# A Swin attention block on one core: other Gelu piece sizes and hidden buffers in its last stage, and output additions moved to GpSimd

## The chip, the cores and the metric

The kernel runs on one core of a Trainium2 chip. The metric is the device time of one execution in microseconds (us). The profile of one execution gives, beside it, the span from the first to the last instruction, and every instruction's start and duration. Engines are called by their short names: PE is TensorE (PEld its weight load), ACT is ScalarE, DVE is VectorE, POOL is GpSimd, SP is the engine that issues nearly all transfers.

## The reference

The input is 8 images of 16 x 128 tokens with 32 channels. The block is one layer of a shifted-window transformer:

```python
y = roll(layernorm(x, g1, b1), (-2, -2))          # then windows of 4 x 32 tokens
q, k, v = (xw @ qkv_w + qkv_b)                     # 4 heads of 8
attn = softmax(q k^T * scale + bias + mask)
x = x + unroll((attn v) @ proj_w + proj_b)
z = layernorm(x, g2, b2)
z = gelu(z @ fc1_w + fc1_b) @ fc2_w + fc2_b        # 32 -> 128 -> 32
return x + z
```

The last three lines, for each image, are what the end stage computes.

## The kernel before

X holds the whole input as 128 partitions (the tokens of a window) by 8 images of 512 columns (16 windows x 32 channels). Attention runs over 64 pairs of windows (8 an image). Every engine has its own instruction list, written out by hand, and executes it in order; semaphores order the engines against each other. The second layer norm and the MLP follow.

The second norm of an image is: row sums (`sums`, L471), a mean (L477), `center` (L495, `xc` = X - mean), `square` (`sq`), sums of squares (L483), a variance (L489), `power` on POOL (L376, var ^ -0.5), `scale` (`yn` = `xc` * `rstd`, L504 on DVE, L386 on POOL) and `channels_second` (L563, a 32 x 32 block transpose into `yT2`). Images 0 to 6 are normalized while attention still runs. Image 7 can be normalized only after its last attention output is added: `add_attention(15)` (L546), which follows PE's `tokens_first(15)` (L1018), DVE's `normalize` and `copy_onT`, and PE's `channels_first(15)` (L1024) and `project_out(15)` (L1030). The number is that of an octet of windows, two octets an image.

The end stage, for image m:

- `fc1(m)` (L951): four matmuls on PE, each one row group of 32 partitions into a PSUM bank of 512 columns, so 2048 hidden columns. Three pairs of banks (`ps1`, `pq`, `ps2`) take turns as halves of 1024 columns. It waits for the Gelu of the first half of image m-1.
- `gelu(m, half)` (L735): ACT reads a pair of banks and writes 1024 columns of `hT[m % 2]`, one of two hidden buffers in memory that attention used before (`q_rows`, `k_rows`). It is preceded once by a table load.
- `fc2(m)` (L967): four matmuls on PE into one bank, `pav` for even and `pch` for odd images; for image 7 two halves of 256 columns into `pq`.
- `mlp_tokens(m)` (L552): DVE transposes the bank into `m_tok`, a single buffer.
- `add_residual(m)` (L558): DVE adds X (which POOL's `add_mlp_bias`, L411, has made X + fc2_b) into `res[m % 2]`, one of two output buffers.
- SP writes `res` to memory (L318, image 7 in halves at L321). `add_residual(m)` waits until the transfer of image m-2 has landed (`d_out[m % 2]`).

PE's order at the end is: `tokens_first(15)`, `fc1(1)`, `channels_first(15)`, `fc2(0)`, `project_out(15)`, `fc1(2)`, `fc2(1)`, then `fc1(m)`, `fc2(m-1)` for m from 3 on. DVE's is: `mlp_tokens(0)` and the normalization of image 7, with `add_residual(0)` and `mlp_tokens(1)` in its middle where it waits for POOL's square; then transpose and addition of one image after the other, `channels_second(7)` behind image 3.

Of the kernel before, what the change touches and what calls it, by code (L numbers as in the profile page):

```python
# [28 lines left out]
LEAD = 4  # L29
AV_LAG = 2  # L30
NPROB = 4


_WIDTHS = dict(g1=1, b1=1, qkb=1, qks=1, colscale=128, wqk=128, ident=128, id3=32,
# [9 lines left out]
def swin_kernel(nc, x, params, rel_i_in, rel_j_in, aux_in, scratch, rel_scratch, out):  # L44
# [3 lines left out]
    with ExitStack() as ctx:  # L48
        def sb(name, shape, dt=fp32):
            return ctx.enter_context(nc.sbuf_tensor(name, shape, dt))  # L50

        def sem(name):
            return ctx.enter_context(nc.semaphore(name))
# [49 lines left out]
        rec = sb("rec", [128, 32])  # L103
        onorm = sb("onorm", [128, 256])
        onT = sb("onT", [128, 256])
        m_tok = sb("m_tok", [128, 512])
        res = sb("res", [128, 2, IMG])

        hT = [t[:, 2, :].bitcast(fp32) for t in (q_rows, k_rows)]

        def psum(name, cols):
            return ctx.enter_context(nc.psum_tensor(name, [128, cols], fp32))

        ps1, ps2, pq = psum("ps1", 1024), psum("ps2", 1024), psum("pq", 1024)
        pav, pch = psum("pav", 512), psum("pch", 512)
        Q0, Q1 = pq[:, 0:512], pq[:, 512:1024]
        FC1 = (ps1, pq, ps2)

        def first_home(j):
            return ps2 if j in (1, 3) else ps1  # L120

        def mlp_home(m, lo):
            return (pav, pch)[m % 2] if m < B - 1 else (Q1 if lo else Q0)


        d_x = [sem(f"d_x{b}") for b in range(B)]
# [27 lines left out]
        onTp_done, onT_done, proj_done, x2_done = (sem("onTp_done"), sem("onT_done"), sem("proj_done"),  # L154
                                                   sem("x2_done"))
        fc1_done, gelu_done, fc2_done = sem("fc1_done"), sem("gelu_done"), sem("fc2_done")
        mtok_done, res_done = sem("mtok_done"), sem("res_done")

        rel_raw, rel_rest = prob[:, 2, 0:512], prob[:, 3, 0:512]

# [2 lines left out]
        def after(eng, s, count):  # L163
            if count > 0:
                eng.wait_ge(s, count)
# [39 lines left out]
        def _(sp):  # L205
# [108 lines left out]
                        gather(n, MID, 0)  # L314
                        gather(n, MID, 1)
            for m in range(B - 1):
                sp.wait_ge(res_done, m + 1)
                sp.dma_start(out[:, m * IMG:(m + 1) * IMG], res[:, m % 2, :]).then_inc(d_out[m % 2], 16)  # L318
            for half in range(2):
                sp.wait_ge(res_done, B + half)  # L320
# [7 lines left out]
        def _(pool):  # L328
# [125 lines left out]
                if p == PAIRS:  # L454
                    add_mlp_bias(B - 2)

            square(second_norm(B - 1))
            power(second_norm(B - 1))
            scale(second_norm(B - 1))
            add_mlp_bias(B - 1)  # L460


        @block.vector
        def _(dve):
# [67 lines left out]

            def normalize(q):
                dve.wait_ge(otok_done, q + 1)
                o = pch[:].rearrange("p (n c) -> p n c", c=16)
                after(dve, on_done, q)
                dve.reciprocal(rec[:].unsqueeze(2), o[:, :, HD:HD + 1]).then_inc(rec_done, 1)
                dve.wait_ge(rec_done, q + 1)
                dve.tensor_tensor(onorm[:].rearrange("p (n d) -> p n d", d=HD), o[:, :, 0:HD],
                                  rec[:].unsqueeze(2).to_broadcast([128, 32, HD]), ALU.mult).then_inc(on_done, 1)  # L540

            def add_attention(q):
                dve.wait_ge(proj_done, q + 1)
                dve.wait_ge(xpb_done, q // 2 + 1)
                xs = img(q // 2).rearrange("p (g t c) -> p t g c", g=NG, t=GW)[:, 2 * (q % 2):2 * (q % 2) + 2]
                dve.tensor_tensor(xs, xs, pch[:, 0:256].rearrange("p (t g c) -> p t g c", t=2, g=NG),  # L546
                                  ALU.add).then_inc(x2_done, 1)

            def mlp_tokens(m, lo=0, hi=512):
                dve.wait_ge(fc2_done, m + 1 + lo // 256)  # L550
                after(dve, res_done, m)
                dve.transpose(m_tok[:, lo:hi], mlp_home(m, lo)[:, lo:hi]).then_inc(mtok_done, 1)  # L552

            def add_residual(m, lo=0, hi=512):
                dve.wait_ge(mtok_done, m + 1 + lo // 256)
                dve.wait_ge(xmb_done, m + 1)
                after(dve, d_out[m % 2], 16 * (m // 2))
                dve.tensor_tensor(res[:, m % 2, lo:hi], m_tok[:, lo:hi], img(m)[:, lo:hi], ALU.add).then_inc(res_done, 1)  # L558

            def channels_second(m):  # L560
                i, seq = second_norm(m)
# [66 lines left out]
            def copy_onT(q):  # L628
                dve.wait_ge(onTp_done, q + 1)
                dve.wait_ge(proj_done, q)  # L630
                dve.tensor_copy(onT[:], pch[:, 0:256]).then_inc(onT_done, 1)

            for p in range(PAIRS):
                b, s = p // PPI, p % PPI
# [34 lines left out]
            copy_oT(OCTETS - 1)  # L669
            normalize(OCTETS - 1)  # L670
            copy_onT(OCTETS - 1)
            mlp_tokens(0)
            add_attention(OCTETS - 1)
            dve.wait_ge(x2_done, OCTETS)
            means(second_norm(B - 1), B - 1)
            center(second_norm(B - 1), B - 1)
            add_residual(0)
            mlp_tokens(1)
            variances(second_norm(B - 1))
            add_residual(1)  # L680
            for m in range(2, B - 1):
                mlp_tokens(m)
                add_residual(m)
                if m == B - 5:
# [7 lines left out]
        def _(act):  # L692
# [39 lines left out]
            def gelu(m, half):  # L732
                act.wait_ge(fc1_done, 2 * m + half + 1)
                after(act, fc2_done, m - 1)
                act.activation(hT[m % 2][:, 1024 * half:1024 * (half + 1)], FC1[(2 * m + half) % 3][:], ACT.Gelu,  # L735
                               bias=f_bias[:]).then_inc(gelu_done, 1)

            act.dma_start(par[:, 0:PSPLIT], params[:, 0:PSPLIT]).then_inc(d_par[0], 16)
            act.wait_ge(zero_ready, 1)
# [75 lines left out]
                    square(second_norm(b - 1))  # L815

            for m in range(B):
                gelu(m, 0)
                gelu(m, 1)


        @block.tensor
        def _(pe):
# [115 lines left out]
            def fc1(m):  # L939
                pe.wait_ge(yT2_done, m + 1)  # L940
                if m == 0:
                    pe.wait_ge(max_done, PAIRS)
                    pe.wait_ge(mmid_done, GROUPS)
                    pe.wait_ge(va_done, B)
                else:
                    pe.wait_ge(gelu_done, 2 * m - 1)
                if m == 1:
                    pe.wait_ge(exp_done, PAIRS)
                for wx in range(GW):
                    bank = FC1[(2 * m + wx // 2) % 3][:, 512 * (wx % 2):512 * (wx % 2 + 1)]  # L950
                    mm = pe.matmul(bank, w1[32 * wx:32 * (wx + 1), :], yT2[32 * wx:32 * (wx + 1), m, :], start=True,  # L951
                                   stop=True)
                    if wx % 2 == 1:
                        mm.then_inc(fc1_done, 1)

            def fc2(m):
                pe.wait_ge(gelu_done, 2 * m + 2)
                if m == 0:
                    pe.wait_ge(oT_done, OCTETS)
                elif m == 1:  # L960
                    pe.wait_ge(x2_done, OCTETS)
                elif m < B - 1:
                    pe.wait_ge(mtok_done, m - 1)
                parts_of = ((0, 512),) if m < B - 1 else ((0, 256), (256, 512))
                for lo, hi in parts_of:
                    for wx in range(GW):
                        mm = pe.matmul(mlp_home(m, lo)[32 * wx:32 * (wx + 1), lo:hi], P("w2"),  # L967
                                       hT[m % 2][:, 512 * wx + lo:512 * wx + hi], start=True, stop=True)
                    mm.then_inc(fc2_done, 1)

            pe.wait_ge(w_ready, 1)
# [42 lines left out]
            def tokens_first(q):  # L1014
                pe.wait_ge(oT_done, q + 1)
                after(pe, x2_done, q)
                for u in range(4):
                    mm = pe.transpose(pch[:, 128 * u:128 * (u + 1)], oT[:, 128 * u:128 * (u + 1)], P("ident"))  # L1018
                mm.then_inc(otok_done, 1)

            def channels_first(q):
                pe.wait_ge(on_done, q + 1)
                for t in range(2):
                    mm = pe.transpose(pch[:, 128 * t:128 * (t + 1)], onorm[:, 128 * t:128 * (t + 1)], P("ident"))  # L1024
                mm.then_inc(onTp_done, 1)

            def project_out(q):
                pe.wait_ge(onT_done, q + 1)
                for t in range(2):
                    mm = pe.matmul(pch[:, 128 * t:128 * (t + 1)], onT[:, 128 * t:128 * (t + 1)], P("wp"),  # L1030
                                   start=True, stop=True)
                mm.then_inc(proj_done, 1)

# [55 lines left out]
            tokens_first(OCTETS - 1)  # L1089
            fc1(1)  # L1090
            channels_first(OCTETS - 1)
            fc2(0)
            project_out(OCTETS - 1)
            fc1(2)
            fc2(1)
            for m in range(3, B):
                fc1(m)
                fc2(m - 1)
            fc2(B - 1)


def _to_tokens(x):
# [105 lines left out]
```

## Time and profile before

| | |
|---|---|
| device time, median of 3 runs | 233.18 us (231.56 to 233.75) |
| device time of the profiled execution | 231.92 us |
| its span, first to last instruction | 230.1 us |
| busy share of the span | PE 90%, DVE 72%, ACT 64%, POOL 56% |
| granted TensorE clock, mean | 0.992 |

The profiled execution took 231.92 us, of which 230.1 us are its span and 1.8 us lie around it. All times in the rows below count from the start of that span. A row of the timeline gives start, duration, engine, line, operation, tiles written and read, and what ended the idle time before it.

### The profile page before, as it was taken

The numbers are of one execution on the slowest core, as the hardware profiler recorded it, in microseconds if no ns is written. First come the engines' busy times: TensorE is split into PE (matmuls) and PEld (weight loads), VectorE is DVE, ScalarE is ACT, GpSimd is POOL, SyncE is SP. The second block draws the span as 40 slices with busy tenths as digits, with TensorE's granted clock in tenths as the row PEclk, the third lists the DMA queues.
The fourth block names the chain that finished last, engine by engine and source line by source line (L and its number), as shares of the span: only waits on it lengthen the run. The fifth ranks groups of instructions, "written<-read, shape, count | busy, mean of one in ns | idle before, by whom it ended". The sixth has DMA issues, their size and how long they took to land.

```text
span 230.1 us, 8103 instructions
## 1 busy us (share of the span) xinstructions
PE 208.0 (90%) x3338; PEld 117.6 (51%) x3338; DVE 165.2 (72%) x254; ACT 148.4 (64%) x216; POOL 128.2 (56%) x116
## 2 busy tenths in 40 slices
PE   0878878799999999999999999999999999979881
PEld 0834424456565566655665566565556555453210
DVE  3896746576776777878787876786756767857865
ACT  7475355565775677677757675867546554677881
POOL 7765688272447956794788397632732091241830
PEclk9999979999999999999999999999999999999999
DMA  6826345545415532442264045305620000000323
GB/s 193 252 65 178 107 161 175 177 162 166 141 56 164 162 101 95 148 157 80 94 187 141 10 140 181 101 11 163 185 74 4 6 6 4 4 0 0 137 105 125
DMA packets 24284, 25.41 MB, mean 110 GB/s; under 512 B 3556, under 2 KB 21732, under 8 KB 24164
## 3 DMA queue, kind: packets, MB, share of 16 engines
q1 hardware_dynamic: 23784, 24.42, 33.6%
q8 instruction: 26, 0.43, 0.7%
q10 hardware_dynamic: 464, 0.48, 0.7%
q14 instruction: 10, 0.08, 0.1%
HBM read 16.24 MB, written 8.39 MB: 107 GB/s over the span
## 4 chain that ended last, share of the span: by engine, by line
issue 40%; POOL 35%; PE 8%; DVE 4%; ACT 4%; DMA 4%; SPq 1%; ACTq 1%; POOLq 1%; DVEq 0%
POOL rstd L376 17%; POOL X L406 4%; POOL yn L386 3%; POOL xc L368 3%; POOL parts L394 3%; POOL X L411 3%; PE ps L951 2%; DMA slots<-parts 2%; DMA X<-x_tok 2%; ACT q_rows L735 1%; POOL mean L356 1%; ACT k_rows L735 1%; POOL var L362 1%; PE pq L951 1%; ACTq L48 1%
## 5 line engine op out<-in xcount | busy, mean ns | idle before, releaser
L524 DVE TENSOR_REDUCE negm<-ps 128x8 f32<-128x1024 f32 x64 | 78.1, 1223 | 33.3 <-PE ps L887 33.2
L730 ACT ACTIVATE prob<-ps 128x1024 f32<-128x1024 f32 x64 | 65.5, 1023 | 41.4 <-PE ps L914 41.3
L376 POOL TENSOR_TENSOR rstd<-var,neghalf 128x16 f32<-128x16 f32 x16 | 47.4, 2963 | 16.8 <-DVE var L489 15.9
L901 PE MATMUL ps<-rel_j,id_b 96*32 96x512 bf16 x512 | 39.9, 385 | 3.3 <-ACT prob L730 2.2
L934 PE MATMUL pav<-prob,va 128*32 128x128 f32 x1024 | 41.1, 279 | 0.0
L934 PEld LDWEIGHTS pav<-prob,va 128*32 128x32 f32 x1024 | 24.1, 109 | 12.5 <-issue 5.0
L865 PE MATMUL ps<-rel_i,ident_b 64*64 64x512 bf16 x256 | 26.4, 402 | 0.2 <-DVE negm L524 0.2
L914 PE MATMUL ps<-q_rows,k_rows 64*128 64x128 bf16 x512 | 25.4, 219 | 1.1 <-DMA q_rows<-m_mid 1.1
L394 POOL TENSOR_TENSOR parts<-rest,parts 128x512 bf16<-128x512 f32 x15 | 17.3, 1156 | 13.8 <-ACT parts L714 13.8
L887 PE MATMUL ps<-k_rows,q_rows 64*128 64x128 bf16 x512 | 24.8, 216 | 0.0
L914 PEld LDWEIGHTS ps<-q_rows,k_rows 64*128 64x128 bf16 x512 | 14.4, 94 | 16.3 <-issue 14.8
L356 POOL TENSOR_SCALAR mean<-ssum 128x16 f32<-128x16 f32 x11 | 2.8, 257 | 28.9 <-DVE ssum L471 28.6
L725 ACT ACTIVATE m_hi<-pq 16x128 bf16<-16x128 f32 x32 | 8.5, 264 | 16.2 <-PE pq L852 13.7
L887 PEld LDWEIGHTS ps<-k_rows,q_rows 64*128 64x128 bf16 x512 | 16.8, 94 | 0.9 <-issue 0.9
L901 PEld LDWEIGHTS ps<-rel_j,id_b 96*32 96x32 bf16 x512 | 11.8, 96 | 9.9 <-ACT prob L730 7.1
L865 PEld LDWEIGHTS ps<-rel_i,ident_b 64*64 64x64 bf16 x256 | 7.2, 103 | 18.5 <-DVE negm L524 7.9
L530 DVE TENSOR_TENSOR m_mid<-pq,m_hi 16x128 bf16<-16x128 f32 x32 | 8.6, 270 | 8.7 <-ACT m_hi L725 7.4
L386 POOL TENSOR_TENSOR yn<-xc,rstd 128x512 f32<-128x512 f32 x13 | 13.9, 1071 | 1.0
L362 POOL TENSOR_SCALAR var<-vsum 128x16 f32<-128x16 f32 x11 | 2.2, 203 | 20.6 <-DVE vsum L483 20.3
L368 POOL TENSOR_TENSOR xc<-X,mean 128x512 f32<-128x512 f32 x12 | 12.6, 1048 | 1.7 <-DVE yn L504 0.8
L471 DVE TENSOR_REDUCE ssum<-X 128x16 f32<-128x512 f32 x16 | 10.9, 681 | 2.9 <-DMA X<-x_tok 2.6
L515 DVE SCALAR_TENSOR_TENSOR rest<-pq,qk_bias,parts 128x512 f32<-128x512 f32 x12 | 9.0, 746 | 5.1 <-ACT parts L708 5.1
(130 smaller groups left out, 332.9 us busy)
## 6 DMA issues: line engine op xcount, KB each, us to landing
slots<-parts SPq DMA_DIRECT2D x21, 256.0 KB, 2.3
q_rows<-slots SPq DMA_DIRECT2D x42, 128.0 KB
k_rows<-slots SPq DMA_DIRECT2D x42, 128.0 KB
X<-x_tok SPq DMA_DIRECT2D x8, 256.0 KB, 4.1
y_tok<-res SPq DMA_DIRECT2D x7, 256.0 KB, 2.0
q_rows<-m_hi SPq DMA_DIRECT2D x32, 4.0 KB
q_rows<-m_mid SPq DMA_DIRECT2D x32, 4.0 KB
bias_parts<-rel_parts SPq DMA_DIRECT2D x3, 128.0 KB
```

The costliest lines, as they stand in the source:

```text
L368: pool.tensor_tensor(per_window(xc[:, i, :]), per_window(img(n)), mean[:, i, :].unsqueeze(2).to_broadcast([128, WPI, C]), ALU.subtract).th ...
L376: pool.tensor_tensor(rstd[:, i, :], var[:, i, :], neghalf[:], ALU.pow).then_inc(rstd_done[i], 1)
L386: pool.tensor_tensor(per_window(yn[:, i, :]), per_window(xc[:, i, :]), rstd[:, i, :].unsqueeze(2).to_broadcast([128, WPI, C]), ALU.mult).t ...
L394: pool.tensor_tensor(parts[:, n % 2, LOW, u, :], rest[:, u, :], parts[:, n % 2, MID, u, :], ALU.subtract).then_inc(lo_done, 1)
L471: dve.tensor_reduce(ssum[:, i, :], per_window(img(n)), AX.X, ALU.add).then_inc(sum_done[i], 1)
L524: dve.tensor_reduce(dst, first_home(j)[:].rearrange("p (a u n) -> p a u n", u=2, n=TOK), AX.X, ALU.max, negate=True).then_inc(max_done, 1)
L730: act.activation(prob[:, j % NPROB, :], ps2[:], ACT.Exp).then_inc(exp_done, 1)
L865: pe.matmul(home[64 * c:64 * (c + 1), 512 * e:512 * (e + 1)], ident_b[64 * e:64 * (e + 1), 64 * e:64 * (e + 1)], rel_i[64 * e:64 * (e + 1) ...
L887: mm = pe.matmul(home[:, 512 * e + at:512 * e + at + TOK], q_rows[64 * e:64 * e + 64, b % NBUF, rows], k_rows[64 * e:64 * e + 64, b % NBUF ...
L901: pe.matmul(ps2[32 * c:32 * (c + 1), 512 * e:512 * (e + 1)], id3_b[0:96, :], rel_j[0:96, c, e].unsqueeze(2).to_broadcast([96, 2, 2, TOK]), ...
L914: mm = pe.matmul(ps2[:, 512 * e + at:512 * e + at + TOK], k_rows[64 * e:64 * e + 64, b % NBUF, rows], q_rows[64 * e:64 * e + 64, b % NBUF, ...
L934: mm = pe.matmul(pav[32 * h:32 * (h + 1), 128 * (j % 4):128 * (j % 4 + 1)], va[:, b % 2, at:at + 32], prob[:, j % NPROB, src:src + 128], s ...
```

## The change

- Gelu of an image is cut into a piece of 512 columns (1536 to 2047, bank `Q1`, first) and one of 1536 columns (banks `ps1`+`Q0` for even, `ps2`+`pch` for odd images). PSUM becomes one tensor of eight banks; `fc1` uses seven of them, `pav` is the eighth. `fc1_done` is counted once an image.
- Four hidden buffers instead of two (`hT[m % 4]`).
- PE's order: `fc1` runs up to four images ahead of `fc2`; `fc2(m-4)`, `fc1(m)` for m from 4 on, then `fc2(4)` to `fc2(7)`. All of `fc2(0)` to `fc2(4)` and `fc2(6)` write the one bank `pav`, so each waits until DVE has transposed the image before (`mtok_done`); `fc2(5)` writes a bank of `ps1`; image 7 uses `Q0` and the other bank of `ps1`.
- `m_tok` becomes two buffers.
- The last octet's attention output goes through `pav` instead of `pch`; `project_out(15)` stands behind `fc1(2)`.
- The last `square` and `scale` go from POOL to DVE. `scale(7)` and `channels_second(7)` stand behind `add_residual(2)`. POOL does `add_mlp_bias(7)` ahead of the last `power`.
- The additions of images 4, 5 and 6 go from DVE to POOL, with a semaphore of their own (`res_pool`); SP and the later transposes wait for it.

```diff
-        hT = [t[:, 2, :].bitcast(fp32) for t in (q_rows, k_rows)]
+        hT = [t[:, i, :].bitcast(fp32) for i in (2, 0) for t in (q_rows, k_rows)]
...
+        FC1_WIDE, FC1_LAST = (banks[:, 0:1536], banks[:, 2048:3584]), Q1
...
+        def wait_result(eng, m):
+            if m in ON_POOL:
+                eng.wait_ge(res_pool, sum(i <= m for i in ON_POOL))
+            elif m >= 0:
+                eng.wait_ge(res_done, sum(i not in ON_POOL for i in range(m + 1)))
...
             def mlp_home(m, lo):
-            return (pav, pch)[m % 2] if m < B - 1 else (Q1 if lo else Q0)
+            if m == B - 3:
+                return ps1[:, 0:512]
+            return pav if m < B - 1 else (Q0 if lo else ps1[:, 512:1024])
...
-            square(second_norm(B - 1))
+            add_mlp_bias(B - 1)
             power(second_norm(B - 1))
-            scale(second_norm(B - 1))
-            add_mlp_bias(B - 1)
+            for m in ON_POOL:
+                pool.wait_ge(mtok_done, m + 1)
+                pool.wait_ge(xmb_done, m + 1)
+                pool.wait_ge(d_out[m % 2], 16 * (m // 2))
+                pool.tensor_tensor(res[:, m % 2, :], m_tok[:, m % 2, :], img(m), ALU.add).then_inc(res_pool, 1)
...
             def mlp_tokens(m, lo=0, hi=512):
                 dve.wait_ge(fc2_done, m + 1 + lo // 256)
-                after(dve, res_done, m)
-                dve.transpose(m_tok[:, lo:hi], mlp_home(m, lo)[:, lo:hi]).then_inc(mtok_done, 1)
+                wait_result(dve, m - 2)
+                dve.transpose(m_tok[:, m % 2, lo:hi], mlp_home(m, lo)[:, lo:hi]).then_inc(mtok_done, 1)
...
             means(second_norm(B - 1), B - 1)
             center(second_norm(B - 1), B - 1)
-            add_residual(0)
-            mlp_tokens(1)
+            square(second_norm(B - 1))
             variances(second_norm(B - 1))
-            add_residual(1)
-            for m in range(2, B - 1):
+            for m in range(B - 1):
                 mlp_tokens(m)
-                add_residual(m)
-                if m == B - 5:
+                if m not in ON_POOL:
+                    add_residual(m)
+                if m == B - 6:
+                    scale(second_norm(B - 1))
                     channels_second(B - 1)
...
             for m in range(B):
-                gelu(m, 0)
-                gelu(m, 1)
+                gelu(m, 1536, 2048, FC1_LAST)
+                gelu(m, 0, 1536, FC1_WIDE[m % 2])
...
             def fc2(m):
                 pe.wait_ge(gelu_done, 2 * m + 2)
                 if m == 0:
-                    pe.wait_ge(oT_done, OCTETS)
-                elif m == 1:
                     pe.wait_ge(x2_done, OCTETS)
+                elif m == B - 3:
+                    pe.wait_ge(gelu_done, 2 * B - 2)
+                elif m == B - 2:
+                    pe.wait_ge(mtok_done, B - 3)
                 elif m < B - 1:
-                    pe.wait_ge(mtok_done, m - 1)
+                    pe.wait_ge(mtok_done, m)
...
             channels_first(OCTETS - 1)
-            fc2(0)
+            fc1(2)
             project_out(OCTETS - 1)
-            fc1(2)
-            fc2(1)
-            for m in range(3, B):
+            fc1(3)
+            for m in range(4, B):
+                fc2(m - 4)
                 fc1(m)
-                fc2(m - 1)
-            fc2(B - 1)
+            for m in range(4, B):
+                fc2(m)
```

## Rows read from the trace of the kernel before

**Rows 1.** Chain that ended last: start, duration, what; one period of the end stage

```profile
213.58 1.12 ACT k_rows L735
214.70 0.14 issue
214.84 1.14 PE ps L951 x8
215.98 0.02 issue
```

**Rows 2.** Timeline of ACT, the first two and the last two Gelu pieces

```profile
205.69 1.11 ACT L735 ACTIVATE q_rows<-ps,f_bias 128x1024 f32<-128x1024 f32 x1
206.70 1.11 ACT L735 ACTIVATE q_rows<-pq,f_bias 128x1024 f32<-128x1024 f32 x1
...
223.27 2.12 ACT L735 ACTIVATE k_rows<-ps,f_bias 128x1024 f32<-128x1024 f32 x2 [0.31 <-PE ps L951]
```

**Rows 3.** Timeline of PE, from the last attention octet to `project_out(15)`

```profile
206.25 0.66 PE L1018 MATMUL pch<-par,oT 128*128 128x128 f32 x4 [1.17 <-DVE oT L626]
206.90 1.14 PE L951 MATMUL ps<-yT,w_s 32*128 32x512 f32 x8
207.97 0.44 PE L1024 MATMUL pch<-par,onorm 128*128 128x128 f32 x2
208.34 1.07 PE L967 MATMUL pav<-q_rows,par 128*32 128x512 f32 x8
209.34 0.71 PE L1030 MATMUL pch<-par,onT 128*128 128x128 f32 x4
```

**Rows 4.** Timeline of DVE in the end stage

```profile
209.47 0.72 DVE L552 STREAM_TRANSPOSE m_tok<-pav 128x512 f32<-128x512 f32 x1 [0.60 <-PE pav L967]
210.11 0.39 DVE L546 TENSOR_TENSOR X<-X,pch 128x256 f32<-128x256 f32 x1
...
211.47 0.69 DVE L495 TENSOR_TENSOR xc<-X,mean 128x512 f32<-128x512 f32 x1
212.08 0.68 DVE L558 TENSOR_TENSOR res<-m_tok,X 128x512 f32<-128x512 f32 x1
...
213.69 0.69 DVE L483 TENSOR_REDUCE vsum<-sq 128x16 f32<-128x512 f32 x1
214.41 0.17 DVE L489 TENSOR_SCALAR var<-vsum 128x16 f32<-128x16 f32 x1
...
215.29 0.72 DVE L552 STREAM_TRANSPOSE m_tok<-pav 128x512 f32<-128x512 f32 x1
216.04 0.69 DVE L558 TENSOR_TENSOR res<-m_tok,X 128x512 f32<-128x512 f32 x1
...
226.63 0.42 DVE L558 TENSOR_TENSOR res<-m_tok,X 128x256 f32<-128x256 f32 x1
...
227.45 0.42 DVE L558 TENSOR_TENSOR res<-m_tok,X 128x256 f32<-128x256 f32 x1
```

**Rows 5.** Groups of ACT by shape: busy us, mean ns of one, idle before

```profile
L708 ACT ACTIVATE parts<-pq,qk_bias 128x512 bf16<-128x512 f32 x12 | 8.2, 682 | 2.9 <-PE pq L834 2.3
```

**Rows 6.** Timeline of POOL, additions, the square and the last power

```profile
202.83 1.28 POOL L411 TENSOR_TENSOR X<-X,par 128x512 f32<-128x512 f32 x1
212.24 1.42 POOL L401 TENSOR_TENSOR sq<-xc 128x512 f32<-128x512 f32 x1 [8.13 <-DVE xc L495]
214.67 3.29 POOL L376 TENSOR_TENSOR rstd<-var,neghalf 128x16 f32<-128x16 f32 x1 [1.01 <-DVE var L489]
```

**Rows 7.** Groups of POOL by shape

```profile
L368 POOL TENSOR_TENSOR xc<-X,mean 128x512 f32<-128x512 f32 x12 | 12.6, 1048 | 1.7 <-DVE yn L504 0.8
```

**Rows 8.** DMA issues after 225 us: KB each, us from issue to landing

```profile
y_tok<-res SPq DMA_DIRECT2D x1, 256.0 KB, 2.0
y_tok<-res SPq DMA_DIRECT2D x2, 128.0 KB, 1.7
```

**Rows 9.** Timeline of DVE: the scale of image 6

```profile
202.97 1.69 DVE L504 TENSOR_TENSOR yn<-xc,rstd 128x512 f32<-128x512 f32 x1 [1.75 <-POOL rstd L376]
```

More of the change, by code:

```diff
@@ L31 @@
 NPROB = 4
+ON_POOL = (4, 5, 6)
 _WIDTHS = dict(g1=1, b1=1, qkb=1, qks=1, colscale=128, wqk=128, ident=128, id3=32,
@@ L105, in swin_kernel, with chain_home @@
         onT = sb("onT", [128, 256])
-        m_tok = sb("m_tok", [128, 512])
+        m_tok = sb("m_tok", [128, 2, 512])
         res = sb("res", [128, 2, IMG])
-        hT = [t[:, 2, :].bitcast(fp32) for t in (q_rows, k_rows)]
+        hT = [t[:, i, :].bitcast(fp32) for i in (2, 0) for t in (q_rows, k_rows)]
         def psum(name, cols):
             return ctx.enter_context(nc.psum_tensor(name, [128, cols], fp32))
[L114 to L117, printed above, removed]
+        banks = psum("banks", 4096)
+        ps1, pq, ps2 = (banks[:, 1024 * i:1024 * (i + 1)] for i in range(3))
+        Q0, Q1, pch, pav = banks[:, 1024:1536], banks[:, 1536:2048], banks[:, 3072:3584], banks[:, 3584:4096]
+        FC1_WIDE, FC1_LAST = (banks[:, 0:1536], banks[:, 2048:3584]), Q1
         def first_home(j):
             return ps2 if j in (1, 3) else ps1
+        def wait_result(eng, m):
[3 more added lines that the diff above has]
+                eng.wait_ge(res_done, sum(i not in ON_POOL for i in range(m + 1)))
+        def chain_home(q):
+            return pch if q < OCTETS - 1 else pav
         def mlp_home(m, lo):
-            return (pav, pch)[m % 2] if m < B - 1 else (Q1 if lo else Q0)
+            if m == B - 3:
+                return ps1[:, 0:512]
+            return pav if m < B - 1 else (Q0 if lo else ps1[:, 512:1024])
         d_x = [sem(f"d_x{b}") for b in range(B)]
@@ L156, in swin_kernel @@
         fc1_done, gelu_done, fc2_done = sem("fc1_done"), sem("gelu_done"), sem("fc2_done")
-        mtok_done, res_done = sem("mtok_done"), sem("res_done")
+        mtok_done, res_done, res_pool = sem("mtok_done"), sem("res_done"), sem("res_pool")
         rel_raw, rel_rest = prob[:, 2, 0:512], prob[:, 3, 0:512]
@@ L316, in _ @@
             for m in range(B - 1):
-                sp.wait_ge(res_done, m + 1)
+                wait_result(sp, m)
                 sp.dma_start(out[:, m * IMG:(m + 1) * IMG], res[:, m % 2, :]).then_inc(d_out[m % 2], 16)
             for half in range(2):
-                sp.wait_ge(res_done, B + half)
+                sp.wait_ge(res_done, B - len(ON_POOL) + half)
                 sp.dma_start(out[:, (B - 1) * IMG + 256 * half:(B - 1) * IMG + 256 * (half + 1)],
@@ L534, in normalize @@
                 dve.wait_ge(otok_done, q + 1)
-                o = pch[:].rearrange("p (n c) -> p n c", c=16)
+                o = chain_home(q).rearrange("p (n c) -> p n c", c=16)
                 after(dve, on_done, q)
@@ L545, in add_attention @@
                 xs = img(q // 2).rearrange("p (g t c) -> p t g c", g=NG, t=GW)[:, 2 * (q % 2):2 * (q % 2) + 2]
-                dve.tensor_tensor(xs, xs, pch[:, 0:256].rearrange("p (t g c) -> p t g c", t=2, g=NG),
+                dve.tensor_tensor(xs, xs, chain_home(q)[:, 0:256].rearrange("p (t g c) -> p t g c", t=2, g=NG),
                                   ALU.add).then_inc(x2_done, 1)
@@ L557, in add_residual @@
                 after(dve, d_out[m % 2], 16 * (m // 2))
-                dve.tensor_tensor(res[:, m % 2, lo:hi], m_tok[:, lo:hi], img(m)[:, lo:hi], ALU.add).then_inc(res_done, 1)
+                dve.tensor_tensor(res[:, m % 2, lo:hi], m_tok[:, m % 2, lo:hi], img(m)[:, lo:hi], ALU.add).then_inc(res_done, 1)
             def channels_second(m):
@@ L630, in copy_onT @@
                 dve.wait_ge(proj_done, q)
-                dve.tensor_copy(onT[:], pch[:, 0:256]).then_inc(onT_done, 1)
+                dve.tensor_copy(onT[:], chain_home(q)[:, 0:256]).then_inc(onT_done, 1)
             for p in range(PAIRS):
@@ L671, in _ @@
             copy_onT(OCTETS - 1)
-            mlp_tokens(0)
             add_attention(OCTETS - 1)
@@ L730, in exponential, with gelu @@
                 act.activation(prob[:, j % NPROB, :], ps2[:], ACT.Exp).then_inc(exp_done, 1)
[L732 to L736, printed above, removed]
+            def gelu(m, lo, hi, home):
+                act.wait_ge(fc1_done, m + 1)
+                after(act, fc2_done, m - 3)
+                act.activation(hT[m % 4][:, lo:hi], home, ACT.Gelu, bias=f_bias[:]).then_inc(gelu_done, 1)
             act.dma_start(par[:, 0:PSPLIT], params[:, 0:PSPLIT]).then_inc(d_par[0], 16)
@@ L948, in fc1 @@
                     pe.wait_ge(exp_done, PAIRS)
+                    pe.wait_ge(x2_done, OCTETS - 1)
                 for wx in range(GW):
-                    bank = FC1[(2 * m + wx // 2) % 3][:, 512 * (wx % 2):512 * (wx % 2 + 1)]
+                    bank = FC1_WIDE[m % 2][:, 512 * wx:512 * (wx + 1)] if wx < GW - 1 else FC1_LAST
                     mm = pe.matmul(bank, w1[32 * wx:32 * (wx + 1), :], yT2[32 * wx:32 * (wx + 1), m, :], start=True,
                                    stop=True)
-                    if wx % 2 == 1:
-                        mm.then_inc(fc1_done, 1)
+                mm.then_inc(fc1_done, 1)
             def fc2(m):
@@ L967, in fc2 @@
                         mm = pe.matmul(mlp_home(m, lo)[32 * wx:32 * (wx + 1), lo:hi], P("w2"),
-                                       hT[m % 2][:, 512 * wx + lo:512 * wx + hi], start=True, stop=True)
+                                       hT[m % 4][:, 512 * wx + lo:512 * wx + hi], start=True, stop=True)
                     mm.then_inc(fc2_done, 1)
@@ L1017, in tokens_first @@
                 for u in range(4):
-                    mm = pe.transpose(pch[:, 128 * u:128 * (u + 1)], oT[:, 128 * u:128 * (u + 1)], P("ident"))
+                    mm = pe.transpose(chain_home(q)[:, 128 * u:128 * (u + 1)], oT[:, 128 * u:128 * (u + 1)], P("ident"))
                 mm.then_inc(otok_done, 1)
@@ L1023, in channels_first @@
                 for t in range(2):
-                    mm = pe.transpose(pch[:, 128 * t:128 * (t + 1)], onorm[:, 128 * t:128 * (t + 1)], P("ident"))
+                    mm = pe.transpose(chain_home(q)[:, 128 * t:128 * (t + 1)], onorm[:, 128 * t:128 * (t + 1)], P("ident"))
                 mm.then_inc(onTp_done, 1)
@@ L1029, in project_out @@
                 for t in range(2):
-                    mm = pe.matmul(pch[:, 128 * t:128 * (t + 1)], onT[:, 128 * t:128 * (t + 1)], P("wp"),
+                    mm = pe.matmul(chain_home(q)[:, 128 * t:128 * (t + 1)], onT[:, 128 * t:128 * (t + 1)], P("wp"),
                                    start=True, stop=True)
```

## The prediction

> **What bounds the kernel now.** I read the chain of waits backwards first. From 211 us on it alternates between one Gelu piece and one `fc1`: a piece of 1.12 us, 0.14 us until PE starts, `fc1` of 1.14 us, then the piece of the next image [rows 1]. A period is 2.42 us (213.58 to 216.00), while ACT's own work in it is two pieces 1.01 us apart [rows 2], 2.02 us. So each period loses 0.4 us. From 205.69 to the end of the last piece, 223.27 + 2.12 = 225.39 us, are 19.7 us [rows 2]; eight images without a gap would take 8 x 2.02 + 0.1 = 16.3. The gaps cost 3.4 us. Next I read the timelines of PE, DVE and POOL, to see what else is close: PE issues `fc1` and `fc2` 1.07 and 1.00 us apart [rows 3], 2.07 us an image, more than ACT's 2.02. After the last piece comes a fixed tail: `fc2(7)`, two transposes and additions, the last transfer. The last addition ends at 227.45 + 0.42 = 227.87 us [rows 4], and the span 2.23 us later, at 230.1.
>
> **The Gelu loop.** From the 1024-column pieces, 1110 ns long and 1.01 us apart, and the 682 ns of an Identity with bias over 512 columns [rows 5], a column costs 0.83 ns and a piece 0.26 us (0.16 when it follows another). The pieces become 0.68 us (spacing 0.58) and 1.54 us (spacing 1.44), still 2.02 us an image. `fc1(m+1)` may start 0.68 + 0.14 = 0.82 us after image m begins and ends 1.17 us later, at 1.99, just inside 2.02. Taken alone, the loop has no gap left and is bound by PE, 2.07 us. That the 1536-column piece crosses three banks has no row; the nearest are the pieces that cross two, at the same cost a column, so I take nothing; its bounds are a gain or a loss of 0.1 us each.
>
> **What the new order does to image 7.** `fc1(2)` waits for the small piece of image 1. That starts at 208.07 us (`fc1(1)` at 206.90 [rows 3] plus 1.17), so `fc1(2)` starts at 208.9, where PE had stood ready at 208.4. `project_out(15)` is queued behind it and starts at 208.9 + 1.07 = 209.97 instead of 209.34 [rows 3], 0.6 us late. DVE's `add_attention(15)` moves from 210.11 to 210.7, and the centering, 1.36 us behind it [rows 4], to 212.06. Now square, sum of squares and variance follow on DVE at 0.72 us each (0.69 and the step to the next), which ends the variance at 214.3 us. Before, it was at 214.58 [rows 4]: DVE's square gains 0.7 us against POOL's 1.42 [rows 6], the late projection takes 0.6 of that back. `add_mlp_bias(7)` on POOL starts with DVE's square and is held by it; it ends at about 214.6, then the power takes 2.9 to 3.3 us [rows 6], until 217.9 at the latest.
>
> **The new wait, and who stands behind it.** `mlp_tokens(0)` now stands behind all of that in DVE's list. It starts at 214.32 though `fc2(0)` is done at 213.1. `fc2(1)` writes the same bank, so PE waits for that transpose: 214.32 + 0.72 + 0.06 = 215.10, where PE was ready at 214.06. Queued behind it in PE's order is `fc1(5)`, whose banks have been free since 215.0, and for it ACT waits. The sequence, each step by the spacings above and 1.13 us from a `fc2` to its transpose [rows 3, 4]:
> - `fc2(0)` 211.99, `fc1(4)` 212.99, `fc2(1)` 215.10, `fc1(5)` 216.10, so Gelu 5 starts at 217.27 where ACT was free at 216.17: 1.1 us of new gap.
> - `fc2(2)` 217.17, `mlp_tokens(2)` 218.30, `add_residual(2)` 219.05, and 0.61 us later, the spacing of two ready DVE instructions [rows 4], `scale(7)` 219.66, `channels_second(7)` 220.38 to 221.09. The power has been done since 217.9, so only the queue delays these two.
> - `fc1(6)` 218.17, `fc2(3)` 219.24, and PE is ready for `fc1(7)` at 220.24, but `yT2` is there only at 221.15. Gelu 7 starts at 222.32 instead of 221.36: another 1.0 us. It ends at 224.44, against 225.39 before.
>
> So of the 3.4 us of gaps, 0.35 stay ahead of image 1 and 2.1 come back as two new ones, and the last Gelu ends only 1.0 us earlier.
>
> **The tail.** Behind `fc1(7)` PE still has four images of `fc2`: 222.22, 223.22, 224.22, and `fc2(7)` at 225.22, not bound by Gelu 7 but by the queue; before, it could start right behind 225.39. So 0.2 us are gained up to here. But the output side is now later:
> - `mlp_tokens(4)` 223.35 to 224.07, POOL starts the addition of image 4 at 224.15. For an addition of two full fp32 tiles on POOL, whose operands don't repeat, the trace of before has no row. The nearest are 1048 ns with a narrow operand [rows 7], 1.28 us with a repeated row, and 1.42 us for the square, held at its start by a DVE addition [rows 6]. I take 1.28 us, with 1.05 and 1.42 as the ends. It ends at 225.43, and that of image 5, right behind it, at 226.71.
> - A 256 KB transfer lands 2.0 us after its issue [rows 8], so image 5, issued at 226.74 (0.03 us behind the addition), lands at 228.74. `add_residual(7)` writes the same `res` buffer and waits for it: its first half starts at 228.77 instead of 226.63 [rows 4].
> - POOL's addition of image 6 waits in the same way for image 4's transfer (225.47 + 2.0) and runs from 227.50 to 228.78, so that it ends as that half starts.
> - From the first half's addition to the end of the second are 1.24 us (226.63 to 227.87), and then 2.23 to the end of the span: 228.77 + 1.24 + 2.23 = 232.24, that is 2.14 us over 230.1.
>
> The sum for the profiled execution is 231.92 + 2.1 = 234.0 us. The median of before lies 1.26 us above its profiled execution, so my forecast for the median is 233.18 + 2.1 = 235.3 us, +0.9%. With POOL's addition at 1.05 us (two of them on the path, 2 x 0.23) it is +1.7 us, with 1.42 +2.4.
>
> **A rule against it.** The scale of image 6 on DVE took 1.69 us beside POOL's 1.28 us bias addition [rows 6, 9]; an addition of the same shape takes 0.69 us [rows 4]. It ended 0.55 us after POOL's. On the other hand an `add_residual` of 0.69 us ran at 216.04 in the middle of POOL's 3.29 us power, not held [rows 4, 6]. The Trainium skill ("SBUF — State Buffer", Who interferes with whom) says that a DVE instruction with two SBUF inputs and a GpSimd one that reads SBUF exclude each other for the whole instruction. The trace agrees for the wide tiles and not for the power. By the rule the sum would be that of the lock rival below; by the rows it stays.
>
> **The rivals.**
> (a) The output buffers or the queue behind image 7's norm don't bite. If the norm were done in time, PE would run at 2.07 us an image: `fc1(7)` 219.2, `mlp_tokens(4)` 221.4, POOL's addition of image 5 ends at 224.7, it lands at 226.8, end of the span 230.3 (226.8 + 1.24 + 2.23), +0.2 us: 233.4. Even a gap-free Gelu buys nothing, as the POOL additions and the landing take it. For it speaks that four hidden buffers let ACT run ahead; against it DVE's order, which admits no overtaking.
> (b) If moreover the transfers didn't hold image 7, the tail would start from `fc2(7)` at 223.3: against 225.4, -2.1 us: 231.1. This is the case of a real gain. Against it stand the 2.0 us landing and only two `res` buffers.
> (c) Slower than my forecast: two additions on POOL cost more than 1.28 us, each holding the next. Image 5's addition starts behind image 4's, and 6's runs when `add_residual(7)` wants the same port, as in [rows 6, 9]. At 1.45 us each it adds 0.35 us in the chain and 0.3 us for the held first half, +2.75: 235.9. It decides from 1.37 us an addition on. For it speaks that neither operand repeats; against it, that the nearest free row is 1.28.
> (d) The lock: `add_residual(0)` at 215.07 would be held until the power ends at 217.9 and end at 218.45; `mlp_tokens(1)` moves from 216.2 to 218.4, PE with it, and the total is +4: 237.2. The row at 216.04 speaks against it.
>
> **How the numbers follow.** Chances: forecast (+1.7 to +2.4) 0.5, (a) 0.1, (b) 0.05, (c) 0.31, (d) 0.04. A measurement of this kernel can tell about 1%, 2.3 us, from no change. Forecast cases lie mostly below +2.3, about one in eight above it: slower by over 1% is 0.31 + 0.04 + 0.06 = 0.41, within 1% is 0.1 + 0.44 = 0.54, faster 0.05. Range: from rival (a), less 0.2 for the three-bank piece, 233.2, to (c) and half of the way to (d), 236.6.
>
> **What would show it.** In the changed profile: ACT idle about 1.1 us before the piece of image 5 and 1.0 us before image 7's, elsewhere next to nothing; `fc2(1)` waiting for DVE's `mlp_tokens(0)`, `fc1(7)` for `channels_second(7)`; POOL additions of 1.05 to 1.42 us; the last but one addition on DVE waiting for the transfer of image 5, about 2 us. The forecast is wrong if DVE finds image 7's norm done much earlier than 214.3 us, if transfers of `res` land much sooner than 2.0 us, or if POOL's additions lie outside 1.05 to 1.42.

## The result, and the profile after

Over 20 runs each, the median is 237.09 us for the changed kernel (233.85 to 240.77) and 233.99 us for the kernel before (231.43 to 238.44). Each kernel's runs spread by about 3%, and the ratio leaves out disturbed runs, the profiled one of the changed kernel among them: 1.0103, with a 95% interval from 1.0058 to 1.0148. The change costs 1.0%, 2.4 us by this ratio; the medians of all runs lie 3.1 us apart. The profiled execution after took 239.11 us with a span of 237.3, 7.2 us more than before. Most of that lies ahead of the change, so the comparison below counts from a common point.

**Where the time came from.** The page's slices of the granted clock, changed kernel:

```profile
PEclk9996799979999999999999999999999999999997
```

The clock dips in slices 4, 5 and 9, and then is at 90% or more in every slice but the last. The busy times by stretch (span part, then each engine's busy us, the granted clock, DMA share and GB/s) say the same:

```profile
0.00:40.00 40.00, 29.10 (x253) 16.52 (x257) 25.89 (x47) 22.59 (x35) 26.79 (x32) 0.91 0.49 147
40.00:80.00 40.00, 36.37 (x633) 22.16 (x634) 25.88 (x36) 23.90 (x37) 18.89 (x19) 0.96 0.46 142
```

In the profile before, the same two stretches were granted 0.96 and 1.00. The instructions there are the same in both kernels, yet the first Gelu piece starts at 210.32 us instead of 205.69 [rows 2]. Those 4.6 us are not the change's: a reduction of DVE in attention (`negm`) starts at 50.56 us before and the same one at 55.19 after, 4.63 us later, and one near the end of attention at 191.93 and 196.56, still 4.63 us apart. What the change touches runs from the first Gelu piece to the end of the span. I call it the **end stage**: 230.1 - 205.69 = 24.41 us before, 237.3 - 210.32 = 26.98 us after, +2.57. It is the yardstick for all that follows.

The timeline of ACT after, one line for the two pieces of an image each (the shape named is that of the first, small one):

```profile
210.32 2.12 ACT L749 ACTIVATE q_rows<-banks,f_bias 128x512 f32<-128x512 f32 x2
212.67 2.12 ACT L749 ACTIVATE k_rows<-banks,f_bias 128x512 f32<-128x512 f32 x2 [0.24 <-PE banks L965]
214.70 2.12 ACT L749 ACTIVATE q_rows<-banks,f_bias 128x512 f32<-128x512 f32 x2
216.73 2.12 ACT L749 ACTIVATE k_rows<-banks,f_bias 128x512 f32<-128x512 f32 x2
218.81 2.12 ACT L749 ACTIVATE q_rows<-banks,f_bias 128x512 f32<-128x512 f32 x2
222.27 2.12 ACT L749 ACTIVATE k_rows<-banks,f_bias 128x512 f32<-128x512 f32 x2 [1.34 <-PE banks L965]
224.34 2.12 ACT L749 ACTIVATE q_rows<-banks,f_bias 128x512 f32<-128x512 f32 x2
227.32 2.12 ACT L749 ACTIVATE k_rows<-banks,f_bias 128x512 f32<-128x512 f32 x2 [0.87 <-PE banks L965]
```

An image takes 2.03 to 2.08 us from start to start where ACT does not wait, against 2.42 before [rows 1]. Beside 0.24 us before image 1, two gaps are left, 1.34 us before image 5 and 0.87 before image 7. The last Gelu ends 19.12 us behind the first's start, against 19.70 before. So ACT's part is 0.6 us shorter, and the end stage 2.6 us longer.

What made the two gaps, from PE's timeline after: `fc2(1)`, with the `fc1(5)` queued behind it, and `fc1(7)`:

```profile
220.07 1.06 PE L982 MATMUL banks<-k_rows,par 128*32 128x512 f32 x8 [1.33 <-DVE m_tok L567]
221.06 1.14 PE L965 MATMUL banks<-yT,w_s 32*128 32x512 f32 x8
...
226.11 1.14 PE L965 MATMUL banks<-yT,w_s 32*128 32x512 f32 x8 [0.85 <-DVE yT L578]
```

And the end of the chain of waits after:

```profile
229.11 0.37 POOL res L475
229.49 0.87 issue
230.35 1.27 POOL res L475
231.63 0.02 issue
231.65 2.01 DMA y_tok<-res
...
234.60 0.43 DVE res L573
```

POOL's addition of image 4, then that of image 5, then image 5's transfer of 2.01 us, and only then image 7's first half on DVE:

```profile
233.78 0.42 DVE L573 TENSOR_TENSOR res<-m_tok,X 128x256 f32<-128x256 f32 x1 [1.60 <-DMA y_tok<-res]
```

The last addition ends at 235.03 and the span 2.27 us later, against 2.23 before.

### The profile page after: what moved, and what is told of

Same layout as the page of the kernel before. It is cut to its first block, busy times and chain, and to the rows that moved or that the text cites. A ratio compares the mean times of both kernels' runs of the same rounds, so it can differ in the third digit from the quotient of the medians.

```text
span 237.3 us, 8099 instructions
## 1 busy us (share of the span) xinstructions
PE 211.0 (89%) x3338; PEld 120.3 (51%) x3338; DVE 165.0 (70%) x253; ACT 148.2 (62%) x216; POOL 129.3 (55%) x117
## 4 chain that ended last, share of the span: by engine, by line
PE 74%; DVE 8%; SPq 5%; DMA 4%; issue 4%; ACT 3%; POOL 2%; DVEq 0%; ACTq 0%
PE banks L947 13%; PE banks L914 11%; PE banks L878 9%; PE banks L927 8%; PE banks L900 6%; PE banks L1045 4%; PE banks L853 4%; PE banks L1033 3%; SPq L262 3%; PE banks L847 3%; PE banks L991 3%; PE banks L865 2%; PE banks L1039 2%; PE banks L965 2%; DMA X<-x_tok 2%
## 5 line engine op out<-in xcount | busy, mean ns | idle before, releaser
L539 DVE TENSOR_REDUCE negm<-banks 128x8 f32<-128x1024 f32 x64 | 78.2, 1224 | 36.5 <-PE banks L900 36.3
L744 ACT ACTIVATE prob<-banks 128x1024 f32<-128x1024 f32 x64 | 65.5, 1023 | 42.9 <-PE banks L927 42.9
L914 PE MATMUL banks<-rel_j,id_b 96*32 96x512 bf16 x512 | 39.5, 381 | 2.4 <-ACT prob L744 2.2
L947 PE MATMUL banks<-prob,va 128*32 128x128 f32 x1024 | 41.2, 279 | 0.0
L947 PEld LDWEIGHTS banks<-prob,va 128*32 128x32 f32 x1024 | 24.1, 109 | 12.6 <-issue 5.3
L927 PE MATMUL banks<-q_rows,k_rows 64*128 64x128 bf16 x512 | 25.6, 220 | 3.0 <-DMA q_rows<-m_mid 3.0
L878 PE MATMUL banks<-rel_i,ident_b 64*64 64x512 bf16 x256 | 26.9, 411 | 0.2 <-DVE negm L539 0.2
L900 PE MATMUL banks<-k_rows,q_rows 64*128 64x128 bf16 x512 | 25.7, 222 | 0.0
L927 PEld LDWEIGHTS banks<-q_rows,k_rows 64*128 64x128 bf16 x512 | 14.5, 95 | 18.1 <-issue 14.7
L900 PEld LDWEIGHTS banks<-k_rows,q_rows 64*128 64x128 bf16 x512 | 17.3, 96 | 1.5 <-issue 1.5
```

What stands on the lines that cost most here:

```text
L539: dve.tensor_reduce(dst, first_home(j)[:].rearrange("p (a u n) -> p a u n", u=2, n=TOK), AX.X, ALU.max, negate=True).then_inc(max_done, 1)
L878: pe.matmul(home[64 * c:64 * (c + 1), 512 * e:512 * (e + 1)], ident_b[64 * e:64 * (e + 1), 64 * e:64 * (e + 1)], rel_i[64 * e:64 * (e + 1) ...
L900: mm = pe.matmul(home[:, 512 * e + at:512 * e + at + TOK], q_rows[64 * e:64 * e + 64, b % NBUF, rows], k_rows[64 * e:64 * e + 64, b % NBUF ...
L914: pe.matmul(ps2[32 * c:32 * (c + 1), 512 * e:512 * (e + 1)], id3_b[0:96, :], rel_j[0:96, c, e].unsqueeze(2).to_broadcast([96, 2, 2, TOK]), ...
L927: mm = pe.matmul(ps2[:, 512 * e + at:512 * e + at + TOK], k_rows[64 * e:64 * e + 64, b % NBUF, rows], q_rows[64 * e:64 * e + 64, b % NBUF, ...
L947: mm = pe.matmul(pav[32 * h:32 * (h + 1), 128 * (j % 4):128 * (j % 4 + 1)], va[:, b % 2, at:at + 32], prob[:, j % NPROB, src:src + 128], s ...
```

## The experiments

Each is one profiled execution unless it says otherwise, read by its end stage (24.41 us before, 26.98 after). Where a ratio is given, it comes from five rounds beside the kernel before. What an experiment does not touch came back closely: the gap before image 5 was 1.34, 1.35 and 1.35 us in the three kernels that share it, the one before image 7 0.86 or 0.87 in eight.

**Eight output buffers.** The changed kernel, `res` with a buffer for each image and no wait for a landing:

```diff
-        res = sb("res", [128, 2, IMG])
+        res = sb("res", [128, B, IMG])
...
-                pool.wait_ge(d_out[m % 2], 16 * (m // 2))
-                after(dve, d_out[m % 2], 16 * (m // 2))
```

> The changed kernel with eight output buffers instead of two: no addition waits for a transfer any more. The yardstick is the end stage, from the start of the first Gelu piece to the end of the span: 24.41 us in the profile of before, 26.98 in the profile of the changed kernel. Theory (the last addition waits for image 5's transfer, 1.6 us of idle time): the first half of the last addition starts 1.6 us earlier, the end stage is 25.3 us. Rival (the wait only hides another limit, POOL's addition queue or PE's fc2 queue): it stays above 26.5 us. The two gaps of ACT before images 5 and 7 stay as they are, 1.3 and 0.9 us.

Measured: 25.87 us, gaps of 1.35 and 0.86. The wait for image 5's transfer was a real cost; 1.1 of its 1.6 us come back. Where the rest went, DVE and POOL timelines of this kernel:

```profile
232.01 0.91 DVE L571 TENSOR_TENSOR res<-m_tok,X 128x256 f32<-128x256 f32 x1
```
```profile
228.92 3.73 POOL L474 TENSOR_TENSOR res<-m_tok,X 128x512 f32<-128x512 f32 x3 [6.82 <-DVE m_tok L566]
```

The first half of the last addition, 0.42 us before and after, takes 0.91. It starts while POOL's third addition runs, and ends at 232.92, 0.27 us behind POOL's (228.92 + 3.73 = 232.65). Without the landing the two engines collide.

**Additions back on DVE.** The changed kernel with one line edited:

```diff
-ON_POOL = (4, 5, 6)
+ON_POOL = ()
```

> The changed kernel with the additions of images 4 to 6 back on DVE, nothing else. Theory (POOL's 1.25 us additions, one behind the other, delay image 5's transfer and so the last addition): image 5 is added 0.5 us earlier, end stage 26.4 us instead of 26.98. Rival (DVE becomes the bound with seven transposes and additions of 1.36 us an image): 27 us or more.

Measured: 26.42 us, as expected. Image 5 is added 0.51 us earlier (20.79 us behind the first Gelu instead of 21.30), and what is left of the wait for its transfer is 0.30 us. POOL's additions are worth 0.56 us of the loss.

**The transpose of image 0 ahead of the variance.**

```diff
             square(second_norm(B - 1))
+            mlp_tokens(0)
             variances(second_norm(B - 1))
             for m in range(B - 1):
-                mlp_tokens(m)
+                if m:
+                    mlp_tokens(m)
```

> The changed kernel with the transpose of image 0 moved ahead of the variance of image 7 on DVE, nothing else. Theory (fc2(1) waits for that transpose, and fc1(5) and Gelu 5 stand behind it): ACT's gap before image 5 shrinks from 1.34 to 0.2 us or less and the end stage from 26.98 to 25.8 us. Rival (the gap is PE's queue of fc1 and fc2 or the norm itself): the gap before image 5 stays, or moves whole to image 7 because the norm is 0.65 us later, end stage over 26.7 us.

Measured: 25.78 us. The gap before image 5 is gone but for 0.18 us:

```profile
217.60 2.12 ACT L751 ACTIVATE k_rows<-banks,f_bias 128x512 f32<-128x512 f32 x2 [0.18 <-PE banks L967]
```

The gap before image 7 stays at 0.86. One DVE instruction behind another cost 1.2 us. In this is the hold of the variance, tested further below: the variance now starts at 215.85, when POOL's bias addition has ended (213.97 + 1.79 = 215.76), takes 0.17 us, and `fc2(1)` no longer stands behind it.

**POOL's additions in the kernel before.** One part of the change alone: two `m_tok` buffers and the additions of images 4 to 6 on POOL.

```diff
+ON_POOL = (4, 5, 6)
...
-        m_tok = sb("m_tok", [128, 512])
+        m_tok = sb("m_tok", [128, 2, 512])
...
                 mlp_tokens(m)
-                add_residual(m)
+                if m not in ON_POOL:
+                    add_residual(m)
```

> The kernel before with one part of the change alone: two transposed buffers and the additions of images 4 to 6 on POOL. Theory (in the old pace of 2.42 us an image POOL's 1.25 us additions and the 2.0 us transfers are done before the last addition needs them): end stage 24.4 us as before, within 0.2. Rival (POOL's additions cost in any case): 25 us or more.

Measured: 24.47 us. At 2.42 us an image, additions on POOL cost nothing. In the changed kernel they cost 0.56 us. What differs there is that four `fc2` follow each other at 0.9 to 1.1 us, closer than POOL's additions of 1.25 us; that this is the reason is read from the timelines, no run changes it alone.

**The projection ahead of `fc1(2)`.**

```diff
-            fc1(2)
             project_out(OCTETS - 1)
+            fc1(2)
```

> The changed kernel with project_out(15) back ahead of fc1(2) on PE, nothing else. Theory (the late projection makes image 7's norm late, and with it the transpose of image 0 and fc2(1)): add_attention(15) starts 1.0 us earlier, Gelu 2 0.7 us later (its gap moves there), Gelu 5 waits 0.1 us instead of 1.34, and the end stage, from the start of the first Gelu piece to the end of the span, is 26.3 us instead of 26.98. Rival (the order costs nothing, since something else holds fc2(1)): 27 us or more, as Gelu 2 is late and nothing is won.

Measured: 26.25 us. Three lines of ACT's timeline:

```profile
214.07 2.12 ACT L749 ACTIVATE q_rows<-banks,f_bias 128x512 f32<-128x512 f32 x2 [0.55 <-PE banks L965]
...
220.25 2.12 ACT L749 ACTIVATE k_rows<-banks,f_bias 128x512 f32<-128x512 f32 x2
...
225.30 2.12 ACT L749 ACTIVATE k_rows<-banks,f_bias 128x512 f32<-128x512 f32 x2 [0.87 <-PE banks L965]
```

Image 2 now waits 0.55 us, image 5 not at all, and the end comes 0.7 us earlier. `add_attention(15)` starts 3.92 us behind the first Gelu instead of 5.00.

**The bias addition behind the power.**

```diff
-            add_mlp_bias(B - 1)
             power(second_norm(B - 1))
+            add_mlp_bias(B - 1)
```

> The changed kernel with POOL's bias addition of image 7 behind the last power instead of ahead of it. In the changed kernel the variance on DVE, 128 x 16, took 0.42 us instead of 0.17, and POOL's bias addition beside it 1.79 us instead of 1.28. Theory (the two engines hold each other): the variance takes 0.17 us, the bias addition 1.28, and the end stage is 0.25 us shorter, 26.7 us. Rival (the 0.42 us is the variance's own in this place): it stays at 0.42, end stage 26.98.

Measured: 26.75 us. DVE's variance after, and then in this kernel:

```profile
218.88 0.42 DVE L504 TENSOR_SCALAR var<-vsum 128x16 f32<-128x16 f32 x1
```
```profile
215.21 0.17 DVE L504 TENSOR_SCALAR var<-vsum 128x16 f32<-128x16 f32 x1
```

And POOL's bias addition beside the variance, after:

```profile
217.48 1.79 POOL L423 TENSOR_TENSOR X<-X,par 128x512 f32<-128x512 f32 x1 [8.74 <-DVE xc L510]
```

The variance is back at 0.17 us and 0.23 us of the end stage with it. The bias addition took 1.53 us, not 1.28, as DVE's additions now run beside it, but nobody waits for it there.

**Both waits removed.** Eight `res` and eight `m_tok` buffers and the early transpose, additions of 4 to 6 still on POOL.

> The changed kernel with eight output and eight transpose buffers and the transpose of image 0 ahead of the variance of image 7; additions of images 4 to 6 on POOL as in the change. Theory (both losses are separate and add up, and POOL's last addition holds the first half of DVE's last one): end stage 23.9 us, 0.5 under before's 24.41. Rival (one wait hides the other): 25 us or more.

Measured: 24.85 us; the expected 23.9 was 0.95 too low. The two gains measured singly, 1.11 and 1.20 us, would give 26.98 - 2.31 = 24.67 us, so in the end stage they add up to within 0.2. DVE's last addition and POOL's three in this kernel:

```profile
231.16 1.01 DVE L570 TENSOR_TENSOR res<-m_tok,X 128x256 f32<-128x256 f32 x1
```
```profile
227.97 3.92 POOL L474 TENSOR_TENSOR res<-m_tok,X 128x512 f32<-128x512 f32 x3 [5.04 <-DVE m_tok L565]
```

The addition takes 1.01 us for 256 columns and ends at 232.17, 0.28 us behind POOL's third at 231.89. That is 21.82 us behind the first Gelu, against 24.71 after: 2.9 us are gained up to here. But the span ends 3.0 us behind the last addition, not 2.23: SP issues in order, image 6's transfer is issued only at 231.91, when POOL's third addition is done, and the two of image 7 behind it. These 0.8 us are most of the miss.

**One addition more on POOL.** As the kernel above, with

```diff
-ON_POOL = (4, 5, 6)
+ON_POOL = (2, 4, 5, 6)
```

> As the kernel with eight buffers and the early transpose, and the addition of image 2 on POOL as well (images 2, 4, 5 and 6), so that DVE reaches image 7's scale 0.6 us earlier. Theory: ACT's gap before image 7 shrinks from 0.9 to about 0.2 us, the end stage is 23.1 us, 1.3 under before's, so 0.5% faster than before. Rival (POOL, with four additions, becomes the bound): 24.4 us or more, no faster than before.

Measured: 25.43 us, ratio 0.9988 (0.9946 to 1.0031). The expectation was wrong by 2.3 us. It was made before the 24.85 us of the kernel above were known, from the 23.9 that were 0.95 us too low; the rest is the gap before image 7, which was to shrink from 0.9 to 0.2 us and grew to 1.44. POOL's addition of image 2 and DVE's scale of image 7, both released by the end of the last power or just behind it:

```profile
220.54 1.28 POOL L474 TENSOR_TENSOR res<-m_tok,X 128x512 f32<-128x512 f32 x1
```
```profile
220.65 1.72 DVE L518 TENSOR_TENSOR yn<-xc,rstd 128x512 f32<-128x512 f32 x1 [0.18 <-POOL rstd L388]
```

POOL was 0.1 us earlier, and DVE took 1.72 us instead of 0.68 on the path to `fc1(7)`: the pattern of [rows 6, 9] again. Rows of before had this price, and I left it out of this sum.

**Without a collision.** Eight buffers of each, the early transpose, and the list of DVE arranged around POOL's two additions:

```diff
+ON_POOL = (4, 5)
...
                 if m == B - 6:
                     scale(second_norm(B - 1))
                     channels_second(B - 1)
+                if m not in ON_POOL and m < B - 2:
+                    add_residual(m)
             for half in range(2):
                 mlp_tokens(B - 1, 256 * half, 256 * (half + 1))
+            add_residual(B - 2)
+            for half in range(2):
                 add_residual(B - 1, 256 * half, 256 * (half + 1))
```

> The kernel with eight buffers and the early transpose, arranged so that DVE and POOL don't add at the same time: POOL adds images 4 and 5 only, DVE transposes 6 and 7 first and adds them behind that, and image 7's scale and transpose stand ahead of the addition of image 2. Theory (the 24.85 us of the kernel before it were lost where POOL and DVE, each with two inputs from SBUF, held one another, and where image 6's transfer came last but two): end stage 23.3 us, 1.1 under before's 24.41, so a ratio of 0.995. Rival (the end stage is bound by PE's queue or by the transfers at the end): 24.4 us or more.

Measured: 23.89 us, an end stage 0.52 us shorter than the kernel before's and 3.09 us shorter than the changed kernel's. The ratio to the kernel before is 0.9941 (0.9885 to 0.9998), and the medians of all runs are 234.34 us for this kernel (12 runs) and 233.94 for the kernel before (17), so the whole time barely tells the two apart; 0.5 us of 234 are 0.2%. Three things differ from the kernel of 24.85 us, and they were not tried singly: 0.45 us of the 0.96 come from the smaller gap before image 7, 0.17 from there to the last addition, 0.34 behind it. The additions at the end are unheld, the gap before image 7 is 0.41 us:

```profile
227.29 1.32 DVE L570 TENSOR_TENSOR res<-m_tok,X 128x512 f32<-128x512 f32 x3
```

Three additions in 1.32 us. Of the 0.6 us over the expected 23.3, 0.46 are at the very end: the last addition ends at 228.61 and the span at 231.3, 2.69 us later, against 2.23 before. Three transfers, 512 KB, are issued within 1.0 us there, and the landing of the last two takes 2.1 us instead of 1.7.

**All additions on DVE, without waits.** Eight buffers of each, the early transpose, `ON_POOL = ()`.

> Eight output and transpose buffers, the early transpose of image 0, and all additions on DVE: no POOL instruction beside DVE's last ones. DVE then needs 1.36 us an image for transpose and addition from image 4 on. Theory (DVE is the bound of the tail then, but nothing holds it): end stage 24.9 us, as with POOL's additions that collide (24.85). Rival (the collisions cost less than thought): 25.5 us or more.

Measured: 24.84 us, as expected. DVE is bound by its 1.36 us an image; POOL with collisions gave the same 24.85. The kernel without them, at 23.89, is not that kernel with one thing changed, as it also scales image 7 earlier.

## Why the prediction was right

The forecast was +2.1 us, +0.9%, and the chances leaned to within 1% (0.54) over slower (0.41). The ratio of 1.0103 lies just across that line. The mechanism came out as forecast; the size did less well: by the end stage the change costs +2.57 us, above the +1.7 to +2.4 that I gave the forecast and nearer to the +2.75 of rival (c). What tells the two apart is the price of POOL's additions, not the total. Step by step, with the predicted times moved by 4.63 us to the common first Gelu:

| step | predicted | after |
|---|---|---|
| `fc1(2)` on PE | 213.5 | 213.50 |
| `add_attention(15)` | 215.3 | 215.32 |
| `mlp_tokens(0)` | 218.95 | 219.22 |
| `fc2(1)` | 219.73 | 220.07 |
| Gelu 5 (gap) | 221.90 (1.1) | 222.27 (1.34) |
| `fc1(7)` | 225.78 | 226.11 |
| Gelu 7 (gap) | 226.95 (1.0) | 227.32 (0.87) |
| POOL, image 5 done | 231.34 | 231.62 |
| addition 7, first half | 233.40 | 233.78 |
| end of span | 236.87 | 237.3 |

- **The Gelu loop**: right. The piece across three banks costs nothing extra: the pair takes 2.12 us, as two pieces of 1024 did [rows 2].
- **The new wait on PE**: right in place, and shown by two edits that start from either end of it: an earlier transpose (-1.20 us) and an earlier projection (-0.73). Both shrink the same gap, so the two gains should overlap; no run has both edits.
- **The variance**: this is the mis-sized term. I let POOL's bias addition be held by DVE's square, but gave DVE's variance its 0.17 us. It took 0.42 us, and ended with POOL's addition (217.48 + 1.79 = 219.27 against 219.30). With that removed, 0.23 of the 0.43 us between the predicted +2.14 and the measured +2.57 are gone. The rest is in steps of 0.1 us or less: 0.85 instead of 0.78 us from the transpose's start to PE, 0.1 from the landing to DVE, 0.04 at the end.
- **POOL's additions**: right. They took 1.25 to 1.27 us, beside the 1.28 that the sum used. Rival (c), slower additions that decide from 1.37 us on, did not happen, and `add_residual(7)` beside the third was not held either (0.42 us).
- **The output buffers**: right. Both the 2.01 us landing and its effect were as forecast, and rival (a) fell in both its forms: the wait bit, and so did the queue behind the norm.
- **Rival (a)'s and (b)'s arithmetic** was too kind, though: with the buffers and the early transpose the end stage was 24.85 us, not the 22.3 of (b): a gap of 0.86 us is left before image 7, and behind the buffers stand the collision of POOL's additions with DVE's and the late issue of image 6's transfer.
- **The lock** of rival (d) did not hold for the power: `add_residual(0)` ran 0.69 us at 219.96, inside POOL's power of 219.38 to 222.29. For wide tiles the two engines do hold each other, in both orders: DVE took 1.72 us instead of 0.68 where POOL was first, POOL 1.79 instead of 1.28 where DVE was. The Trainium skill ("SBUF — State Buffer", Who interferes with whom) also counts a DVE `tensor_scalar` among those that can contend; the trace agrees, with 0.42 against 0.17 us. By it the variance waits until POOL's addition ends, and that is when it ended; my sum left this out.

By the ratio the forecast's base of 233.18 us becomes 233.18 x 1.0103 = 235.6 us, against 235.3 forecast. The raw median of 237.09 us lies above my range of 233.2 to 236.6. The end stage explains 2.6 of the 3.1 us between the medians; ahead of it the profiles differ by more than the rest. The first Gelu starts between 205.3 and 210.4 us in the twelve profiles of this case, and it goes with the clock granted in the first and the second 40 us: 205.3 and 205.7 at 0.96 and 1.00, 206.6 and 206.8 at 0.91 and 1.00, 207.4 to 208.0 at 1.00 and 0.96, 208.8 and 209.1 at 0.87 and 1.00, 210.1 to 210.4 at 0.91 and 0.96. That the rest of the higher median is due to this is not shown, as only one of each kernel's 20 runs has a profile.

## What to carry to other kernels

When an engine that bounds a loop is freed of its gaps, write down the in-order lists of all other engines against the new, faster times: here one transpose queued behind a norm cost 1.2 us and one addition that had to wait for a transfer 1.1, and with both removed the end stage was 24.85 us, still no shorter than the 24.41 of before. An output buffer that is free in time at the old pace is not at a new one; count issue to landing, 2 us, against the distance between its writers. And count pairs of instructions on DVE and POOL that both read from SBUF at the same time: their order of arrival decides who waits, and moving work to the idle engine can lengthen the busy one's path, here by up to 1 us an instruction (1.72 instead of 0.68).

## What the runs showed of the hardware that was not expected

- A DVE `tensor_scalar` of only 128 x 16 elements, with one tensor input, is held by a POOL addition: 0.42 us, against 0.17 with POOL idle. The same instruction for the mean, 2.4 us earlier and with POOL idle, took 0.17.
- A DVE addition that starts inside a POOL one ends 0.27 us behind it for 256 columns (232.92 against 232.65). POOL's power does not hold one: 0.69 us at 219.96, inside 219.38 to 222.29.
- Three transfers, 512 KB, issued within 1.0 us at the end go with a way from the last addition to the end of the span of 2.69 us instead of 2.23, and of 3.0 us in the kernel where image 6's is issued at 231.91 and the last addition ends at 232.17.
- The granted clock in the first 80 us differs from run to run (0.87 to 1.00 in the first 40 us, 0.96 to 1.00 in the next) with the same instructions, and the start of the end stage moves with it by up to 5 us, twice what the change does.
